# Attention outputs re-laid channel-major through DRAM in place of transposes on TensorE, with the softmax inverses taken on 64 columns

## The reference

```python
        attn = jax.nn.softmax(scores, axis=-1)
        out = jnp.einsum('bhqk,bhkd->bhqd', attn, V)
        out = out.transpose(0, 2, 1, 3).reshape(B, N, D)
        return out @ wo.T
```

## Time and profile before

| | us |
|---|---|
| median of 3 runs (1382.7 to 1386.96) | 1385.34 |
| the profiled execution | 1386.62 |
| its span | 1384.8 |
| PE busy in it | 1218.0 |
| DVE busy in it | 932.8 |

### The profile page before, as it was taken

How to read it: one execution, slowest core, us unless ns; L and a number is a source line. 1 busy time by engine, 2 the same in 40 slices (tenths; PEclk the granted TensorE clock), 3 DMA queues, 4 the chain that set the end, 5 groups by cost and what they waited for, 6 DMA issues and landing times.

```text
span 1384.8 us, 26785 instructions
## 1 busy us (share of the span) xinstructions
PE 1218.0 (88%) x8190; PEld 650.1 (47%) x8190; DVE 932.8 (67%) x2502; ACT 710.5 (51%) x1300; POOL 269.9 (19%) x557
## 2 busy tenths in 40 slices
PE   3446999999889998999999999999999979999876
PEld 1222233333356655445555555556666535455445
DVE  5877778687455555767778776755554476668676
ACT  2221776777644434566666666663222227666643
POOL 3342211111000012322332332110000211222112
PEclk7557999999999998999999999999999989999988
DMA  7312232310000003323333222100000202221000
GB/s 207 124 65 73 87 90 68 120 35 19 1 1 1 0 1 120 105 66 107 106 98 126 74 78 76 45 4 3 1 0 0 74 12 67 77 81 40 2 1 31
DMA packets 65200, 79.16 MB, mean 57 GB/s; under 512 B 5483, under 2 KB 58068, under 8 KB 64602
## 3 DMA queue, kind: packets, MB, share of 16 engines
q1 hardware_dynamic: 65098, 77.89, 18.1%
HBM read 45.27 MB, written 31.72 MB: 56 GB/s over the span
## 4 chain that ended last, share of the span: by engine, by line
PE 62%; issue 13%; DVE 9%; ACT 4%; DMA 4%; DVEq 3%; POOL 2%; SPq 1%; POOLq 1%; ACTq 0%
PE bank L1606 11%; PE bank L1620 11%; PE bank L1590 9%; PE bank L1772 6%; PE bank L1773 6%; PE bank L1790 5%; PE bank L1574 3%; PE bank L1608 2%; DVE M L1189 2%; DMA KS<-scr_k 2%; PE bank L1640 2%; DVE masked_scores L1186 1%; PE bank L1510 1%; DVE N L1026 1%; PE bank L1570 1%
## 5 line engine op out<-in xcount | busy, mean ns | idle before, releaser
L912 ACT ACTIVATE PT<-bank 128x512 f32<-128x512 f32 (+1 forms) x784 | 427.5, 569 | 246.9 <-PE bank L1608 176.2
L1590 PE MATMUL bank<-KS,QS 125*128 125x512 bf16 (+3 forms) x1024 | 308.6, 329 | 31.5 <-DVE M L1186 12.1
L1606 PE MATMUL bank<-QS,KS 128*128 128x512 bf16 (+3 forms) x1024 | 303.7, 323 | 15.2 <-ACT PT L912 8.0
L1189 DVE TENSOR_REDUCE M<-bank 128x1 f32<-128x512 f32 (+2 forms) x400 | 257.8, 684 | 87.9 <-PE bank L1590 52.2
L1186 DVE CUSTOM_DVE_ANT_0 masked_scores<-bank,maskw 128x384 bf16<-128x384 f32 (+1 forms) x384 | 228.7, 622 | 90.0 <-PE bank L1590 78.8
L1620 PE MATMUL bank<-PT,VA 128*32 128x512 f32 (+3 forms) x2048 | 211.5, 485 | 1.6 <-ACT PT L912 1.0
L1606 PEld LDWEIGHTS bank<-QS,KS 128*128 128x128 bf16 x1024 | 99.3, 98 | 215.5 <-ACT PT L912 152.4
L1590 PEld LDWEIGHTS bank<-KS,QS 125*128 125x128 bf16 x1024 | 100.6, 99 | 109.0 <-DVE M L1189 31.9
L1608 PE MATMUL bank<-identb,maskw 128*128 128x128 bf16 x768 | 147.7, 219 | 0.0
L1790 PEld LDWEIGHTS bank<-MW,PT 128*128 128x128 f32 x864 | 111.7, 193 | 40.8 <-issue 38.2
L1772 PE MATMUL bank<-XT,MW 128*128 128x512 f32 (+1 forms) x232 | 120.7, 602 | 10.1 <-DVE PT L1363 5.9
(11 more groups left out here) (229 smaller groups left out, 1522.6 us busy)
## 6 DMA issues: line engine op xcount, KB each, us to landing
scr_q<-PQ SPq DMA_DIRECT2D x48, 384.0 KB, 3.2
QS<-scr_q SPq DMA_DIRECT2D x64, 288.0 KB
scr_k<-PK SPq DMA_DIRECT2D x24, 384.0 KB, 3.6
KS<-scr_k SPq DMA_DIRECT2D x32, 288.0 KB
QS<-MSB SPq DMA_DIRECT2D x192, 4.0 KB
MW<-in_m_w SPq DMA_DIRECT2D x3, 1024.0 KB, 9.5
MW<-in_m_w SPq DMA_DIRECT2D x3, 832.0 KB
scr_k<-PK SPq DMA_DIRECT2D x24, 96.0 KB, 1.9
```

The costliest lines, as they stand in the source:

```text
L912: a.activation(PT[kt % 2][:, js[0]:js[-1] + 1, q0:T], tiles(bank[st_bank(L, g, i)][:, 0:w * len(js)], len(js)), ACT.Exp, scale=c["scale"]) ...
L1189: v.tensor_reduce(M[g % 2][:, t * GH + js[0]:t * GH + js[-1] + 1], tiles(bank[S_ORDER[L][i]][:, 0:kl * len(js)], len(js)), AX_X, ALU.max, ...
L1590: r = mm(s, QS[0:ROWS_SHIFT, g * GH + j, t * P:(t + 1) * P], KS[0:ROWS_SHIFT, kv_slot(L, g, j), 0:kl], start=True, stop=not by_pe)
L1606: r = mm(s, KS[:, kv_slot(L, g, j), kt * P:(kt + 1) * P], QS[:, g * GH + j, T - w:T], start=True, stop=not causal)
```

## The change

In all blocks but the last of a chain (`relaid`, 13 of 16) the turning by TensorE is gone. `store_o` writes OT as it is to DRAM (`scr_o`), `load_o` reads back only the 8 output rows of each head, channel-major, into OU, and the 16 rows of sums spread over 128 partitions as 64 columns (`sums`). `recip` takes the inverses on VectorE, `store_recip` writes them, and `load_recip` reads each head's row into 8 partitions (`recips_wide`). `scale_o` multiplies OU and `recips_wide` on GpSimd into AOT. `y_out` moves from unit 1, item 1 to unit 2, item 0, the sum and statistics to unit 2, item 1, and the norms behind them. Last blocks of a chain keep the old way. SyncE's order in a unit is new: for units 2 and 3 the stack is loaded first, and the wait for the stored parts moves into `load_stack`.

```diff
-Y_AT, Y_SUM_AT, Y_STATS_AT = (1, 1), (1, 4), (1, 6)
-
-LATER = dict(norm=(2, 2), stats2=(2, 5), norm2=(3, 3), xt=(3, 6), out=(3, 7))
-EARLIER = dict(norm=(2, 1), stats2=(2, 1), norm2=(2, 3), xt=(2, 6), out=(2, 7))
+RECIP_AT, Y_AT, Y_SUM_AT, Y_STATS_AT = (1, 0), (2, 0), (2, 1), (2, 1)
+
+LATER = dict(norm=(2, 6), stats2=(2, 8), norm2=(3, 4), xt=(3, 6), out=(3, 7))
+EARLIER = dict(norm=(2, 5), stats2=(2, 5), norm2=(2, 5), xt=(2, 8), out=(2, 9))
...
-LOGITS_AT, GATES_AT = {2: 0, 4: 1, 9: 2}, 9
-GATES_T_AT = {5: 0, 7: 1, 9: 2}
+LOGITS_AT, GATES_AT = {2: 0, 4: 1, 10: 2}, (3, 0)
+GATES_T_AT = {9: 0, 11: 1, 13: 2}
...
+def relaid(L, b):
+
+    return not (is_last(b) and any(L == c[-1] for c in CHAINS))
...
-                at_least(sp, parts_stored, (B + 1) * 96)
 
             def load_stack(L, b, g):
+                if g == 0:
+                    at_least(sp, parts_stored, (b + NB * L + 1) * 96)
+                    passed(b)
...
+            def store_o(L, b, g):
+
+                r = relaid_block(L, b)
+                sp.wait_ge(o_evac, U(L, b, g) + 1)
+                passed(b)
+                if g == 0:
+                    at_least(sp, o_landed, r * 32)
+                    passed(b)
+                sp.dma_start(bass.AP(tensor=scr_o, offset=g * P * T, ap=[[T, P], [1, T]]), OT[:, :]).then_inc(o_stored, 16)
+
+            def load_o(L, b):
+
+                r = relaid_block(L, b)
+                sp.wait_ge(o_stored, (r + 1) * NG * 16)
+                passed(b)
+                at_least(sp, o_scaled, r)
+                passed(b)
+                sp.dma_start(sums[:, :], bass.AP(tensor=scr_o, offset=HD * T, ap=[[32 * T, H], [T // HD, HD], [1, T // HD]])).then_inc(o_landed, 16)
+                sp.dma_start(OU[:, :], bass.AP(tensor=scr_o, offset=0, ap=[[32 * T, H], [T, HD], [1, T]])).then_inc(o_landed, 16)
+
+            def store_recip(L, b):
+                r = relaid_block(L, b)
+                sp.wait_ge(recip_done, r + 1)
+                passed(b)
+                at_least(sp, recip_landed, r * 16)
+                passed(b)
+                sp.dma_start(bass.AP(tensor=scr_r, offset=0, ap=[[T // HD, P], [1, T // HD]]), recips[:, :]).then_inc(recip_stored, 16)
+
+            def load_recip(L, b):
+                sp.wait_ge(recip_stored, (relaid_block(L, b) + 1) * 16)
+                passed(b)
+                sp.dma_start(recips_wide[:, :], bass.AP(tensor=scr_r, offset=0, ap=[[T, H], [0, HD], [1, T]])).then_inc(recip_landed, 16)
...
                     if g == 0:
                         load_stack(L, b, 3)
+                    elif g == 1 and end:
+                        store_recip(*end)
+                    elif g >= 2 and ahead:
+                        load_stack(ahead[0], ahead[1], g - 1)
+                    if prev and relaid(*prev[:2]):
+                        store_o(*prev)
                     if follow:
                         load_shift(*follow)
+                    if end and g == 0:
+                        load_o(*end)
                     if prep:
                         store_parts(*prep)
-                        load_stack(*prep, 0)
-                    elif g >= 2 and ahead:
-                        load_stack(ahead[0], ahead[1], g - 1)
+                    next_block = neighbours(L, b, 0)[3]
+                    if g == 1 and next_block:
+                        load_stack(*next_block, 0)
+                    if g == 1 and end:
+                        load_recip(*end)
...
+            def scale_o(L, b):
+
+                r = relaid_block(L, b)
+                wait(o_landed, (r + 1) * 32)
+                wait(recip_landed, (r + 1) * 16)
+                wait(y_ready, b + NB * LAYERS[L]["phase"])
+                g.tensor_tensor(AOT[:, :], OU[:, :], recips_wide[:, :], ALU.mult).then_inc(o_scaled, 1)
...
                     if gg == 1 and end:
+                        scale_o(*end)
+                    if gg == 2 and end:
                         post_root(LAYERS[end[0]]["phase"], end[1])
-                    if gg == 2 and end:
+                    if gg == 3 and end:
...
-            def o_out(L, u, g):
+            def o_out(L, b, u, g):
                 act.wait_ge(pv_done, (u + 1) * NT)
+                if relaid(L, b) or g == 0:
+                    at_least(act, o_stored, (u - ends_before(L) * NG) * 16)
+                else:
+                    act.wait_ge(ot_ready, turned_unit(L, g))
                 a.activation(OT[:, :], bank[4][:, :], ACT.Copy).then_inc(o_evac, 1)
...
-                        if end and g == 0 and i == AO_OUT_AT:
-                            ao_out(*end)
...
+            def recip(L, b):
+
+                r = relaid_block(L, b)
+                dve.wait_ge(o_landed, (r + 1) * 32)
+                at_least(dve, recip_stored, r * 16)
+                v.reciprocal(recips[:, :], sums[:, :]).then_inc(recip_done, 1)
...
-                        if prev and i == O_NORM_AT:
+                        if prev and not relaid(*prev[:2]) and i == O_NORM_AT:
                             o_norm(*prev, u - 1)
+                        if end and (g, i) == RECIP_AT:
+                            recip(*end)
...
-                pe.wait_ge(o_normed, w - 1) if not isinstance(w, int) or w > 1 else None
+                at_least(pe, m_evac, w)
+                if g > 2 and not relaid(L, b):
+                    pe.wait_ge(o_normed, turned_unit(L, g - 3) + 2)
+                elif g == 0 and is_first(b) and starts_chain(L):
+                    pe.wait_ge(o_normed, turned_unit(L, 0) + 1)
...
-                        if prev and i == O_T_AT:
-                            o_t(L, u - 1, u + 2 if follow else u + 1, not follow)
-                        if end and g == 0 and i == AO_T_AT:
-                            ao_t(*end, PREP_BASE[prep[0]] + (prep[1] + 1) * PREP_USES[prep[0]] if prep else PREP_BASE[L] + NB * PREP_USES[L])
+                        if prev and not relaid(*prev[:2]) and i == O_T_AT:
+                            o_t(L, u - 1, g - 1, u + 2 if follow else u + 1, not follow)
                         if end and (g, i) == Y_AT:
-                            pe.wait_ge(ao_evac, end[1] + NB * end[0] + 1)
+                            next_block = neighbours(L, b, 0)[3]
+                            pe.wait_ge(prep_evac, PREP_BASE[next_block[0]] + (next_block[1] + 1) * PREP_USES[next_block[0]] if next_block
+                                       else PREP_BASE[L] + NB * PREP_USES[L])
+                            pe.wait_ge(o_scaled, relaid_block(*end) + 1)
                             y_out(AOT, attn_weights(end[0])[5], end[1], LAYERS[end[0]]["phase"])
```

More of the change, by code:

```diff
@@ L217, in end_at, with ends_before, relaid_block, turned_unit @@
 def end_at(L, b):
-    return EARLIER if is_last(b) and any(L == c[-1] for c in CHAINS) else LATER
+    return EARLIER if is_last(b) and L in GATED_BY else LATER
+def relaid(L, b):
+    return not (is_last(b) and any(L == c[-1] for c in CHAINS))
+def ends_before(L):
+    return sum(c[-1] < L for c in CHAINS)
+def relaid_block(L, b):
+    return b + NB * L - ends_before(L)
+def turned_unit(L, g):
+    return ends_before(L) * NG + g
 def at_least(eng, sem, count):
@@ L290, in build @@
         AO = sb("AO", [P, NT, P])
+        OU = sb("OU", [P, T])
+        sums = sb("sums", [P, H * T // P])
+        recips = sb("recips", [P, H * T // P])
+        recips_wide = sb("recips_wide", [P, T])
         AOT = sb("AOT", [P, T])
@@ L359, in build @@
              "pool_xts", "dma_alibi"))
+        o_stored, o_landed, recip_done, recip_stored, recip_landed, o_scaled = (sem(n) for n in (
+            "dma_o_stored", "dma_o_landed", "dve_recip", "dma_recip_stored", "dma_recip_landed", "pool_o"))
         qm_used, tern_ready = sem("dve_absum_used"), sem("dve_ternary")
@@ L376, in build @@
         scr_k = nc.dram_tensor("scr_k", [H * STACK * T], BF16, kind="Internal").ap().tensor
+        scr_o = nc.dram_tensor("scr_o", [NG * P * T], F32, kind="Internal").ap().tensor
+        scr_r = nc.dram_tensor("scr_r", [H * T], F32, kind="Internal").ap().tensor
         def wc(name):
@@ L502, in _, with passed @@
             sp.dma_start(slope[:, :], d["slopes"]).then_inc(ld_f, 16)
+            def passed(b):
+                if not isinstance(b, int):
+                    sp.sem_inc(sp_passed, 1)
             def store_parts(L, b):
@@ L918, in unit @@
                         if prev and i == O_OUT_AT:
-                            o_out(L, u - 1, g - 1)
+                            o_out(prev[0], prev[1], u - 1, prev[2])
                         if follow and i == SHIFT_T_AT + 1:
                             m_out(*follow)
-                        if end and g == 0 and i == AO_OUT_AT:
-                            ao_out(*end)
                         if end and (g, i) == end_at(L, b)["out"]:
                             xt_out(LAYERS[end[0]]["phase"], end[1])
-                        if L in GATED_BY and is_last(b) and (g, i) == (2, GATES_AT):
```

(13 more changed lines are left out.)

9 lines of the change are left out of this document (4 added, 5 removed).

## The result

The changed kernel took 1420.07 us (median of 4 runs, 1415.44 to 1424.54), the kernel before 1385.3 us: ratio 1.0252, 95% interval 1.0215 to 1.029. It is 35 us slower. The prediction had the sign, but 1393 us and a range that ends at 1408. The profiled execution has a span of 1422.7 us against 1384.8, so 37.9 us are to be found; it is the slowest of the four (1424.54 us), so some 4 of them are not in the median.

What follows compares the result with a forecast made beforehand. TensorE's program was taken to set the pace. Terms -28.6 - 5.9 + 1.4 + 25.4 + 11.4 + 3.0 + 0.9 = +7.6 us on the profiled 1386.6 gave 1394.2, forecast as a median of 1393 us, range 1364 to 1408.

Steps and rivals of the forecast that it cites:

- transposes: TensorE, 13 re-laid blocks: 260 transposes of O and AO removed at 0.11 us each, -28.6 us.
- key stacks: First blocks of layer 1: SyncE's new order removes TensorE's 3.2 us wait; later stack 0 in block 0 costs +1.4.
- shift rows: First blocks of layer 1: TensorE's 2.7 us wait goes, as unit 2's shift is issued ahead of stack 0.
- wait in front of Y: Unit 2: TensorE waits for GpSimd's product behind the load of the inverses, 2.2 us in six blocks, +25.4 us in all.
- VectorE: Unit 2: sum, statistics and norms crowded together hold back scores; +11.4 in two-norm blocks, +3.0 in layer 2, +0.9 in layer 0.
- the rival of the clock: Idleness before Y halves TensorE's clock, up to 1.65 us per fall, 16 in all ten loaded blocks: 1409; chance 0.10.
- The wait in layer 1, block 0: Stack 0 is issued 2 us later than before and lands some 1.4 us after TensorE asks: +1.4 us.
- No wait for key stacks at the head of units 3 and 0: Sign expected in the profile after, in layer 1: TensorE no longer waits for key stacks there.
- the 3.7 taken: Load that spreads the inverses, 256 KB: 3.7 us from issue to landing, taken from a same-size load at the kernel's start.
- The wait at item 5: Unit 2: reduce 2 ends at 5.6, TensorE would issue item 5's score at 4.0; 1.6 us lost.
- the one at the opening of unit 3: Reduce 9 ends at 13.2, TensorE needs it at 9.85 to open unit 3; 3.3 us lost, old order 1.4.

Runs made afterwards that it cites:

- statistics apart, no trip: Changed kernel without store and load of the inverses (outputs not normalised), first statistics at item 4 of unit 2 instead of item 1: 1380.81 us, ratio 0.9929.
- The run without the trip: Changed kernel without the store and load of the inverses, GpSimd multiplying the reloaded outputs by themselves (not normalised): 1381.27 us, ratio 0.9953.
- the filled wait: Changed kernel with 32 unread matmuls in front of the wait for the product, in layers 1 to 3: 1414.02 us, ratio 1.0202.
- the run with the order alone: Kernel before with only SyncE's new order (stacks 1 and 2 heading their units, unit 2's shift rows ahead of stack 0): 1385.03 us, ratio 0.9983.
- Two runs with the steps apart: First statistics at item 4, changed kernel without the inverses' transfers: 0.9929; VectorE's block-end steps spread, changed kernel with Y at item 4, product behind shift: 1.0066.
- the best: Changed kernel with Y at item 4 of unit 2, the product behind the shift on GpSimd, and VectorE's block-end steps spread: 1397.57 us, ratio 1.0066.

## Why the prediction was wrong

The sum had +7.6 us; the spans differ by 37.9. In the order of its terms:

| term | predicted | measured | from |
|---|---|---|---|
| transposes | -28.6 | about -20 of busy time | 1218.0 to 1197.8 (statistics apart, no trip) |
| clock | 0 (rival, 16) | +17 | 1197.8 to 1215.1, same instructions |
| key stacks | -3.2 + 1.4 | +8.5 | waits |
| shift rows | -2.7 | -2.7 | waits |
| wait in front of Y | +25.4 | +26.4 | waits |
| VectorE | +15.3 | +7.6 for M, +2.7 for N | waits |

The measured column sums to about 40; smaller waits (ScalarE's among them) give back 2.

**The step that failed** is the rival of the clock, put at 0.10 and left out of the sum: "Against: the unit with a shorter wait for its shift rows, at 685.07, has a granted clock of 1.00". The trace before has this at that place:

```profile
685.07 0.39 PE L1606 MATMUL bank<-QS,KS 128*128 128x512 bf16 x1 [0.32 <-DMA QS<-MSB]
```

A wait of 0.32 us was no evidence for waits of 2 to 4, least of all when a second one, for the stack, stands 0.4 us of work before. The row that bore on it was the earlier trace rows, 2.44 us of idle and 0.50 behind. By it the forecast would have had the rival's 16 us as a term, 1409; the key stacks make most of the rest, while the transposes (8.6 us too good) and VectorE (5.0 too bad) cancel in part. The run without the trip against the changed kernel (15.3 us of busy time) and the filled wait show the clock's term. The Trainium skill's page TensorE: Matmul & The Clock Gate, section Why this matters for your kernels, says that idle gaps between bursts of matmuls bring the clock back to half; the trace agrees, with 0.53 behind 2.86 us of idle time.

**The key stacks** are the second miss, 10 us. The wait in layer 1, block 0 was foreseen with 1.4 us and came with 2.0; the rest was not. I asked when stack 0 would be issued only for that block, and not when it would be needed: the units ahead of it became shorter by what the change took out of them, and the parts followed only in part. I also took the shift rows ahead of stack 0 for a gain alone. They set when it is issued, 2.8 us ahead of unit 2 on average instead of 6.9, and the run with the order alone has seven such waits. "No wait for key stacks at the head of units 3 and 0" came true; they are waited for at the head of unit 2 instead.

**The transposes** were priced from start to start, 0.11 each. TensorE's queue does pay that at their place, but not the unit: behind them stood waits that they had covered. Alone they are worth 0.046 each in time, by the run with fewer of them. In the changed kernel part of what they free shows up as the waits of the other rows, so the table counts their busy time only. The 20 is the roughest figure there: a little of the 20 can be clock, and the run with fewer transposes gives 15.8 for 222, or 18.5 for 260.

**The wait in front of Y** was right in place, releaser and total, but by errors that cancel. In layer 1, block 1 it was 1.8 and not 3.7 us since TensorE first waited 3.5 for the stack; in layer 3, block 1 it was 4.0 and not 2.2. The median landing was within 0.7 us of the 3.7 taken, as the rows of DMA issues show, first of the changed kernel, then with the load ahead of the stack:

```profile
recips_wide<-scr_r SPq DMA_DIRECT2D x13, 256.0 KB, 4.4
```

```profile
recips_wide<-scr_r SPq DMA_DIRECT2D x13, 256.0 KB, 3.5
```
The Trainium skill's page DMA: Bandwidth & Descriptors, section Anatomy of one DMA, gave 2.6 us, an estimate, for DMAs that GpSimd issues; the shortest of the landings in these two traces is 3.1, and the measured landing decides.

**VectorE's burst** is half its predicted size. The wait at item 5 was counted with 1.6 us and is 0.3 to 1.5 in the two-norm blocks; the one at the opening of unit 3 was counted with 3.3 and is 0.7 to 1.0. Two runs with the steps apart gained nothing that can be told.

What was not shown: the changed kernel with stack 0 ahead of the shift rows, as it stood before, was not run, so what this would give back in time stays open; nor were the moves of the order run one by one. By the landing times, earlier parts alone would not bring stack 0 forward while it stands behind the shift rows. No version here is faster than the kernel before with its full work; the best has 1.0066.

## What to carry to other kernels

Price a wait on TensorE twice: the idle time, and what the half clock behind it makes of the next few microseconds of work; look for the nearest wait of the same length in the trace, not for a shorter one. When work leaves a stretch, ask for every transfer that ends in that stretch whether its producer became faster too; if not, it is the next wait. Ask the same of what now stands ahead of it in its queue. And when an instruction is made to wait for a round trip, move what is queued behind it first: moving its reader alone gained 8 us here, moving it behind its neighbour 16 more.

## What the hardware showed

32 useless matmuls in front of each of ten waits made the program some 7 us faster, with intervals that overlap a little. A unit without scores ahead (layer 2, block 3) fell to a mean clock of 0.71 behind a wait of 1.78 us, while layer 1, block 3 with 0.46 and 1.90 us stayed at 1.00: the length of the gap alone does not tell.
